# Expert slots in an order that the chip makes, weights waited for through ScalarE, and the first pass's transposes a block later

## What is computed

```python
h = layernorm(x)
q, k, v = h @ Wq, h @ Wk, h @ Wv                      # 8 heads of 64
q = softmax(q, over 64) * 0.125; k = softmax(k, over 4096)
out = (k v^T) applied to q, then @ Wo + bo
x = x + layernorm(out)
u = layernorm(x)
s = softmax(u @ centroids.T); top 2 of 16 -> gates g
routed = sum over the two experts of g * (u @ Wr[e].T + br[e])
shared = (u @ Ws[0].T + u @ Ws[1].T + sum(bs)) / 2
x = x + layernorm(u + routed + shared)
```

## Time and profile before

| what | value |
| --- | --- |
| median of 3 runs | 1136.12 us (1130.5 to 1185.25) |
| the profiled execution | 1130.6 us |
| its span, core 5, the slowest | 1128.7 us |
| the other cores' spans | 1099.4 to 1122.9 us |
| TensorE busy, matmuls | 833.8 us, 74% |
| VectorE, ScalarE, GpSimd busy | 587.4, 480.2, 273.7 us |
| mean granted TensorE clock, core 5 | 0.888 |

### The profile page before, as it was taken

One profiled execution on the slowest core, in us unless ns is written; L12 is line 12 of the kernel. 1 busy time (PEld: TensorE's weight loads), 2 busy tenths in 40 slices (PEclk: granted clock), 3 DMA queues, 4 the chain that ended last, 5 costly groups with the idle time before them and its releaser, 6 DMA issues.

```text
span 1128.7 us, 18028 instructions; the slowest of 8 cores (1099.4 to 1128.7 us)
## 1 busy us (share of the span) xinstructions
PE 833.8 (74%) x5008; PEld 410.9 (36%) x5008; DVE 587.4 (52%) x1352; ACT 480.2 (43%) x837; POOL 273.7 (24%) x295
## 2 busy tenths in 40 slices
PE   3797898888676677204377789964798978999994
PEld 1343444444233334102133345531344433444441
DVE  3589776776687888531032122210121233887876
ACT  1453454553676768300011222210121234777775
POOL 0132222213104343655011100010001004544441
PEclk9898999999889788556688999986999997999997
DMA  9999889867858992438979975677969655888885
GB/s 180 247 195 240 200 216 231 219 156 133 176 169 198 273 230 99 163 128 277 214 211 254 234 283 204 213 188 181 274 188 256 247 191 189 276 287 285 280 286 213
DMA packets 74194, 245.07 MB, mean 217 GB/s; under 512 B 9678, under 2 KB 9966, under 8 KB 73484
## 3 DMA queue, kind: packets, MB, share of 16 engines
q0 software_dynamic: 30800, 109.93, 42.6%
q1 hardware_dynamic: 43196, 132.88, 34.5%
HBM read 183.71 MB, written 98.19 MB: 250 GB/s over the span
## 4 chain that ended last, share of the span: by engine, by line
PE 34%; DMA 19%; DVE 18%; issue 10%; DVEq 7%; ACT 5%; ACTq 3%; POOLq 1%; another core or an unknown queue 1%; POOL 1%; SPq 0%
PE pa L1551 17%; DMA xs<-xd 5%; DMA wfull<-wr 4%; PE pa L554 3%; PE pa L480 3%; PE pa L1748 3%; DMA xh<-xin 2%; DMA out<-zo 2%; DVE xh L951 2%; PE pT L1514 2%; DVEq L590 2%; DVEq L356 2%; DMA xd<-ub,pos 2%; DVE acc L1788 1%; DVE acc L1779 1%
## 5 line engine op out<-in xcount | busy, mean ns | idle before, releaser
L1551 PE MATMUL pa<-wfull,xsT 128*128 128x512 bf16 x1200 | 287.8, 396 | 85.2 <-DMA wfull<-wr 49.1
L1583 DVE COPY ro<-pa 128x512 f32<-128x512 f32 x79 | 54.6, 691 | 319.5 <-PE pa L1551 308.2
L1551 PEld LDWEIGHTS pa<-wfull,xsT 128*128 128x128 bf16 x1200 | 116.9, 101 | 226.3 <-issue 111.3
L1582 ACT COPY ro<-pa 128x512 f32<-128x512 f32 x79 | 46.3, 587 | 274.6 <-PE pa L1551 256.4
L1748 PE MATMUL pa<-wfull,uT 128*128 128x512 bf16 x512 | 122.7, 383 | 0.0
L1765 POOL DMA_INDIRECT rr<-yr,ypos x64 | 84.4, 1318 | 155.6 <-issue 86.8
L1204 POOL DMA_INDIRECT xd<-ub,pos x64 | 63.3, 989 | 119.7 <-ACT ub L984 54.5
L918 PE MATMUL pa<-Mb,qT 128*128 128x512 bf16 x256 | 80.8, 446 | 0.0
L1436 POOL DMA_DIRECT2D wfull<-wr x28 | 14.8, 530 | 253.3 <-issue 169.8
L1530 ACT COPY xsT<-pT 128x1024 bf16<-128x1024 bf16 x40 | 40.5, 1013 | 81.0 <-PE pT L1514 78.0
L1514 PE MATMUL pT<-sq,xs 128*128 128x128 bf16 x608 | 47.6, 222 | 32.2 <-DMA xs<-xd 32.2
(11 more groups left out here) (208 smaller groups left out, 1347.9 us busy)
## 6 DMA issues: line engine op xcount, KB each, us to landing
yr<-ro SPq DMA_DIRECT2D x79, 512.0 KB, 4.1
xs<-xd SPq DMA_DIRECT2D x75, 256.0 KB
wfull<-wbf POOLq DMA_DIRECT2D x36, 512.0 KB, 13.6
xh<-xin SPq DMA_DIRECT2D x32, 512.0 KB, 14.7
stg<-wr POOLq DMA_DIRECT2D x32, 512.0 KB, 10.1
wbf<-stg SPq DMA_DIRECT2D x32, 512.0 KB, 10.6
wfull<-wr POOLq DMA_DIRECT2D x32, 512.0 KB, 16.3
out<-zo SPq DMA_DIRECT2D x32, 512.0 KB
```

What stands on the lines that cost most here:

```text
L1551: m = e.matmul(pa[j % 2][:, o * 512:(o + 1) * 512], xsT[j % 2][:, k * P:(k + 1) * P], wfull[:, c:c + 512], start=(k == 0), stop=(k == 7))
L1582: return e.copy(ro[j % 3][:, s], pa[j % 2][:, s])
L1583: return e.tensor_copy(ro[j % 3][:, s], pa[j % 2][:, s])
```

## The change

Line numbers in the order rows of the changed kernel are its own.

1. **Slot order.** The largest expert among 3 to 15 becomes a filler. Its weights stay in buffer 0 behind expert 0's; all others take turns between buffers 1 and 2. The others come in order, and each from the third on whose own slots are fewer than four (VISIT) is followed by so many of the filler's slots; what is left of the filler comes at the end. The table (ZY, TB) has a seventh number, the block of yr to which the slot's result goes, since the gathers still look for results in expert order.
2. **Loads.** One lookup for each slot (WL) in place of three; a float32 load goes out whole. Expert 1's load now stands in the second pass, expert 2's behind its last batches; zeroes for experts 8 to 15 are filled behind slot 0, and the zero tile is set by GpSimd.
3. **Waits for weights.** From slot 8 (NEAR) on ScalarE looks up what slot j + 1 waits for and waits for it (RD), ahead of its copy EO(j, 0); TensorE waits for RD and looks up the buffer alone.
4. **Slot 0** has a fixed place, waits for no table, and its matmuls come before slot 1's transposes.
5. **Stores** look up their block; unused slots store an old tile without waiting for copies. The last pass's first two blocks don't wait for the last stores.
6. **First pass.** TH and EH of the next group stand one V or Q block later, EU behind the third query block's VectorE work.

```diff
+VISIT = 4
+NEAR = 8
...
             TK(g, 2)
             if n:
                 H(n[1])
-                TH(n[0])
             X4(g, 1)
-            if n:
-                EH(n[0])
             EV(t[1])
 
             V(t[2])
             TK(g, 3)
             if n:
-                TH(n[1])
+                TH(n[0])
                 H(n[2])
-                EH(n[1])
+                EH(n[0])
...
             if n:
-                TH(n[2])
+                TH(n[1])
                 H(n[3])
-                EH(n[2])
+                EH(n[1])
...
             QQ(t[0])
             if n:
-                TH(n[3])
-                EH(n[3])
+                TH(n[2])
+                EH(n[2])
...
             QQ(t[1])
             if n:
+                TH(n[3])
+                EH(n[3])
                 E(g)
             else:
...
             QQ(t[2])
-            if n:
-                EU(g)
             QS(t[2])
             QR(t[1])
             QN(t[1])
+            if n:
+                EU(g)
...
+            if b == NB - 1:
+                plan[done].append((ZZ,))
+                plan[done].append((LD0, 2))
...
+            if s == NT - 1:
+                LD0(1)
     def ZZ():
         def zz(e):
-            wait(e, "W", 17)
+            wait(e, "W", NT - 1)
             return e.memset(zero[:], 0.0)
-        put("V", ("ZZ",), zz)
+        put("G", ("ZZ",), zz)
...
-            return e.tensor_copy(zidx[:], tmp)
+            return e.tensor_copy(zidx[:, 0:1], tmp[:, 0:1])
...
+            e.reduce_max(sc[0], key[:, 3:16], axis=AX.X)
...
+            e.tensor_scalar(one, key, sc[0], None, ALU.is_equal)
...
+            e.tensor_scalar(g, T, -1.0, float(VISIT), ALU.mult, ALU.add)
...
+            e.tensor_tensor_scan(hc[:, 3:17], ones16[:, 0:14], g[:, 2:16], 0.0, ALU.mult, ALU.add)
...
+            e.tensor_scalar(hc[:, 3:17], hc[:, 3:17], big_n, None, ALU.min)
...
+            e.scalar_tensor_tensor(tf[:, 1:2], sc[24], 0.0, sc[23], ALU.is_equal, ALU.mult)
+            e.scalar_tensor_tensor(tf[:, 5:6], sc[21], float(CAP), sc[24], ALU.mult, ALU.add)
+            e.scalar_tensor_tensor(tf[:, 6:7], sc[22], sc[24], sc[18], ALU.add, ALU.max)
+            dr()
+            return e.tensor_copy(tabi[:, 0:7], tf[:, 0:7])
         put("V", ("TB",), tb)
...
         def f(e):
             wait(e, "ZX")
             wait(e, "ZZ")
-            if n == 1:
+            if n:
                 wait(e, "TB")
-            if n >= 8:
+            if 8 <= n < NE:
                 wait(e, "ZF", n - 8)
             return [e.indirect_dma_start(
                 out=xd[:], out_offset=bass.IndirectOffsetOnAxis(ap=zidx[:, n:n + 1], axis=0),
                 in_=zero[:], in_offset=None, bounds_check=last_row[0], oob_is_err=False)]
-        put("G", ("ZF", n), f, f"d_zf{n % 8}")
+        put("G", ("ZF", n), f, f"d_zf{n % 8 if n < NE else 8}")
 
     def YP(n):
 
...
+        b = (0, 2, 1)[n]
+
         def f(e):
             if n == 0:
                 wait(e, "W", 15)
             if n == 1:
+                wait(e, "W", NT - 1)
+            if n == 2:
                 wait(e, "SCAT", batch_of[NT - 6])
                 wait(e, "TU", NT - 6)
-            if n == 2:
-                wait(e, "W", NT - 1)
-                for k in range(NE - 8, NE):
-                    wait(e, "ZF", k)
             if n:
                 for q in range(4 * n - 4, 4 * n):
                     wait(e, "PS", q)
-            return [e.dma_start(out=wfull[:, n * WSZ + h * QTR:n * WSZ + (h + 1) * QTR],
+            return [e.dma_start(out=wfull[:, b * WSZ + h * QTR:b * WSZ + (h + 1) * QTR],
                                 in_=(wbf if n else wr)[n][:, h * QTR:(h + 1) * QTR]) for h in range(4)]
-        put("G", ("LD0", n), f, f"d_v{n}" if n else "d_w0", 4)
-
-    def loads_until(n):
-
-        kind = [m for m in range(NE + 1) if (m in PRE or m == NE) == (n in PRE or n == NE)]
-        return sum(m <= n and m % 3 == n % 3 for m in kind)
-
-    def fetch(e, b, src, chan, part):
+        put("G", ("LD0", n), f, f"d_w{b}", 4)
...
-    def WL(j, h):
-
-        def f(e):
-            wait(e, "TB")
-            wait(e, "MM2", j - 1)
-            with from_table(nc, e, "Pool", tabi, j, ((2, NE - 1), (3, 2))) as ((reg, val), (buf, _)):
-                with e.If_ne(reg, 0):
-                    src = wr[bass.ds(val, 1), :, :].rearrange("a p c -> (a p) c")
-                    by_buffer(e, buf, lambda b: fetch(e, b, src, "d_w", (2 * h, 2 * h + 1)))
-        Q.own("G", f)
-
-    def WH(j):
+    def WL(j):
...
-            with from_table(nc, e, "Pool", tabi, j, ((4, NE), (3, 2))) as ((reg, val), (buf, _)):
-                with e.If_ne(reg, 0):
-                    src = wbf[bass.ds(val, 1), :, :].rearrange("a p c -> (a p) c")
-                    by_buffer(e, buf, lambda b: fetch(e, b, src, "d_v", range(4)))
+
+            def load(src, most):
+                with from_table(nc, e, "Pool", tabi, j, ((2, most), (3, 2))) as ((_, val), (buf, _)):
+                    weights = src[bass.ds(val, 1), :, :].rearrange("a p c -> (a p) c")
+                    by_buffer(e, buf, lambda b: fetch(e, b, weights, range(4)))
+            with from_table(nc, e, "Pool", tabi, j, ((2, NE),)) as ((some, _),):
+                with e.If_ne(some, 0):
+                    with from_table(nc, e, "Pool", tabi, j, ((4, 1),)) as ((prepared, _),):
+                        with e.If_eq(prepared, 0):
+                            load(wr, NE - 1)
+                        with e.Else():
+                            load(wbf, NE)
...
-                wait(e, "TB")
                 wait(e, "W", NT - 1)
                 wait(e, "SCAT", NB - 2)
                 wait(e, "SCAT", NB - 1)
+                wait(e, "ZF", 0)
+                return [e.dma_start(out=xs[0][:], in_=xd[0:P, :])]
+            wait(e, "TB")
+            wait(e, "ZF", NE)
             if j < NE:
-                wait(e, "ZF", j)
+                wait(e, "ZF", min(j + 1, NE - 1))
...
+    def arrival(e, j, b, first):
...
+        loads = ([(NE, 2)], [(v + 1, v // 2) for v in range(2, 15, 2)],
+                 [(v + 1, v // 2 + 1) for v in range(1, 14, 2)])[b]
+        for code, m in loads:
+            if code == NE or code <= j + 1:
+                with e.If_eq(first, code):
+                    e.wait_ge(Q.sem[f"d_w{b}"], 64 * m)
+
+    def RD(j):
+
+        def f(e):
+            with from_table(nc, e, "Activation", tabi, j, ((1, NE),)) as ((first, _),):
+                with e.If_ne(first, 0):
+                    with from_table(nc, e, "Activation", tabi, j, ((0, 2),)) as ((buf, _),):
+                        by_buffer(e, buf, lambda b: arrival(e, j, b, first))
+            e.sem_inc(Q.sem["rd"], 16)
+            return []
+        put("A", ("RD", j), f, "rd")
...
-            with e.If_ne(first, 0):
-                for n in range(b, min(NE, j + 1), 3):
-                    with e.If_eq(first, n + 1):
-                        e.wait_ge(Q.sem[f"d_v{b}" if n in PRE else f"d_w{b}"], 64 * loads_until(n))
+            if 0 < j < NEAR:
+                with e.If_ne(first, 0):
+                    arrival(e, j, b, first)
...
-            with from_table(nc, e, "PE", tabi, j, ((0, 3), (1, NE))) as ((buf, _), (first, _)):
+            if j == 0:
+                wait(e, "LD0", 0)
+                both(e, 0, None)
+                return
+            if j == 1:
+                wait(e, "TB")
+            if j >= NEAR:
+                wait(e, "RD", j)
+            cols = ((0, 3), (1, NE)) if j < NEAR else ((0, 3),)
+            with from_table(nc, e, "PE", tabi, j, cols) as regs:
+                buf = regs[0][0]
+                first = regs[-1][0]
...
+                if j == 2:
+                    for n in range(8, NE + 1):
+                        wait(e, "ZF", n)
             else:
                 wait(e, "YS", j - 3)
+            if j >= SURE:
+                wait(e, "EO", j - 3, o)
...
+            cols = ((6, NSLOT - 1), (0, 3)) if j >= SURE else ((6, NSLOT - 1),)
+            with from_table(nc, e, "SP", tabi, j, cols) as regs:
+                def rows():
+                    wait(e, "EO", j, 0)
+                    wait(e, "EO", j, 1)
+                    return e.dma_start(out=yb[bass.ds(regs[0][1], 1), :, :].rearrange("a p d -> (a p) d"),
+                                       in_=ro[j % 3][:])
+                if j < SURE:
+                    return [rows()]
+                seen = dict(Q.seen)
+                with e.If_ne(regs[1][0], 3):
+                    rows().then_inc(Q.sem[ys(j)], 16)
+                with e.Else():
+                    e.dma_start(out=yr[j * P:(j + 1) * P, :], in_=xh[j - SURE][:]).then_inc(Q.sem[ys(j)], 16)
+                Q.seen.clear()
+                Q.seen.update(seen)
+            return []
+        put("S", ("YS", j), f, ys(j))
...
     def experts():
-        for n in range(4):
+        ZF(0)
+        ZF(NE)
+        for n in range(1, 8):
             ZF(n)
-        LD0(1)
```

(25 more changed lines are left out.)

176 lines of the change are left out of this document (106 added, 70 removed).

## The result

The changed kernel takes 1083.7 us (median of 6 runs, 1078.9 to 1128.6), the kernel before beside it 1144.2 (6 runs). Some executions of either kernel are some per cent longer, with the cores of one die at a lower granted clock; the ratio is of the others alone, 0.954, interval 0.950 to 0.958: faster. The profiled execution took 1078.9 us, against 1130.6 before.

The account below looks back on a forecast made before the run. The slowest core, 5, sets the time; its longest stage, the expert slots, was split by transfers. 1130.6 - 8 - 4 - 32 - 5 = 1081.6, said as 1082 us; range 1038 to 1112.

Parts of the forecast that it names:

- Term 1: First pass: transposes a block later remove TensorE's waits for VectorE's normalised block; -8 us, bounds -20 and +5.
- Term 2: Table and first slots: table ready later, at about 503 us, but slot 1 earlier; -4 us, bounds -8 and +5.
- Term 3: Expert stage, slot 1 to last matmul: 402 us falls to 370 by the transfer split; -32 us, bounds -73 and +9.
- the check at expert 9: Expert stage: expert 9's load, needed four slots (15.6 us) after the request, takes 23 us including those slots' traffic.
- Term 4: Hand-over to the last pass: first blocks skip the store waits, GpSimd has fewer lookups; -5 us, bounds 0 and -9.
- ScalarE's lookups at nothing: Expert stage: a lookup is one register load and a branch, costed at nothing beside 1.1 of 3.9 us copying.
- holds the slot: Rival, expert stage: ScalarE's lookup delays the copy out of PSUM, 1.2 us for each of 67 slots; 1162 us, chance 0.07.
- Everything is covered: Rival, expert stage: TensorE bounds and all loads are hidden, -73 us there; 1040.6 us in all, chance 0.20.
- The transfers eat it: Rival: loads cost more, stage gains 0 to 15 us, first pass gains nothing; 1115 us, chance 0.15.
- the slower rival: Expert stage: ScalarE's lookup, at 4 us, adds 80 us over 67 slots; 1162 us, chance 0.07.
- The order isn't what I derived: Rival, slot table: one wrong column makes slots wait for other weights; would show as about 1115 us, no separate chance.

Follow-up runs that it names:

- a1_old_first: Changed kernel with the first pass put back in the old order; 0.982 of the kernel before, first pass 286.9 us against 270.8.
- early: Changed kernel with expert 2's first load moved behind zeroing of experts 1 to 7, and zeroing of experts 8 to 15 moved earlier; 0.958 of the kernel before.
- allbf: Changed kernel with the seven float32 loads fetching bfloat16 weights of the expert below; 0.923 of the kernel before, slots 329.0 us against 364.4.
- noload: Changed kernel without the expert loads behind the first three, every slot using buffer 0; one run, 1007.7 us, slots 292.3 us against 364.4.
- vlook: Changed kernel with the lookup of weights on VectorE instead of ScalarE; 0.958 of the kernel before, slots 366.6 us against 364.4.
- a4_no_visits: Changed kernel with VISIT = 0, all filler slots at the end; 0.987 of the kernel before, slots 395.0 us against 364.4.
- v5: Changed kernel with VISIT = 5 instead of 4; 0.959 of the kernel before, slots 362.8 us against 364.4.
- after_again: The changed kernel unchanged, run in a second batch; 0.956 of the kernel before, slots 365.0 us against 364.4.

## Why the prediction was right, and where not

I predicted 1082 us and it is 1083.7. Three of the four terms are right in kind. Terms 1, 2 and 4 were mis-sized, by -10.6, +5.9 and +2.0 us, and the errors nearly cancel: that the total is so close is in part luck. The forecast's own bounds, half of each term's, add up to 1051 and 1116, not to the 1055 and 1107 that I gave; the range of 1038 to 1112 was a choice beside them.

**Term 1, -8 predicted, -18.6 measured (a1_old_first: 16.1).** The mechanism was right. The step that failed is the size, "two thirds of 12.1": I summed the waits for hb alone, within 40 to 260 us of one core, and took a third off for the transfers. But a wait in an in-order queue also moves what stands behind it. On core 1 hb gave 11.0, the key transposes another 6.9, and the matmuls 3.2 (busy 220.0 to 216.8, fewer of them in slow stretches), less 1.2 for qn: 19.9 of 19.8. On core 5, from which the 12.1 was read, the pass is 14.4 us shorter. The third that transfers were to eat was not seen, and the fourth copy into hT, my bound of +5, made no new wait (1.4 us before and after). The bound of -20, "all waits, the slow matmuls and the stalls behind them", was the better figure.

**Term 2, -4 predicted, +1.9 measured.** The step that failed is that all of it was read from core 5, where the table was late before (44.4 us behind the second pass; 32.4 to 32.6 on cores 0 to 3). On core 5 slot 1 did come 9.3 us earlier. On cores 0 to 3 it came 5.9 us later, 57.4 to 63.3, because there GpSimd's list is the bound and the change put a memset, a load and another zeroing into it: the last scatter is issued 36 instead of 32 us behind the second pass, and slot 0's transposes start at 46.6 instead of 40.8. "Fit the 8.5 us in which GpSimd waited for the last positions" held for core 5 alone. The run early takes this back on such cores and so shows it. The table's own making was over-priced, too: 12.4 us were predicted, and it takes 9.3 to 10.8 by core, where it took 5.9 to 6.2. On core 5 it is ready no later than before, because the last positions came 3.9 us earlier (31.6 us behind the second pass for 35.5), which nothing in the term had foreseen.

**Term 3, -32 predicted, -31.4 measured.** The split holds on core 5, 498 to 865 us: transfers busy 0.84 of 367 us = 308 (307 predicted), the rest 59 (22 + 41 = 63 predicted). Pace and the sum of transfers were right, and so was the time of a load in the check at expert 9: 23 us predicted, and a float32 load with four slots beside it took 20.3 to 22.9 us. That makes a stop of 7.4 us, though, and at slot 26 of core 5, expert 9's, two copies are 16.8 us apart, a stop of 12.9. The prices of the two kinds of load don't follow from the earlier trace rows as written: 20.9 us for one of each and 164 for nine and seven give 8.9 and 12.0, not 7.4 and 13.5. The stated ones were the better: from the software queue's busy time within the slots in allbf (fourteen bfloat16 loads, 96 us without what noload has too) and in the changed kernel (141 us) they come to about 7 and 13. Two readings in the term were off. "Idle for float32 weights falls from 49 to about 40" named the wrong rows: the stop now shows as waits for rows, which share the transfer engines with the load and stand ahead of the matmuls on TensorE. And the stops last longer than their idle time, since the slot behind one runs at 1.2 GHz, 5.91 us for 3.62; I had no term for it. In the one stop shown the transfers were busy all the while (1.01 in 641 to 647 us), so it lies under their time there.

The weighed rule of the Trainium skill, DMA: Bandwidth & Descriptors (SWDGE vs HWDGE vs iDMA), by which a transfer engine takes turns between the software and the hardware queues, gave me 27 us for a float32 load beside full slot traffic. That took the turns to be equal in time. If they are counted in packets the trace agrees with the page: 576 and 590 packets beside that load (544 and 534 beside another, 544 to 562 us), of which the load's last 0.43 and the slots' 0.12 us, so that the load had 77% of the time. The load's own 22.7 us decide nothing: 13.5 + 4 x 2.4 = 23.1 comes out for any turns that let the slots' 9.6 us through before the load has ended. It is the rows' 15.2 to 18.9 us that show how the turns fall.

**Term 4, -5 predicted, -3.0 measured** (-4.2 at the gathers). The last pass's first transposes come 10.7 us after the last slot on core 5 (864.76 to 875.42) instead of 12.4, 1.7 us earlier:

```profile
865.55 0.23 PE L1732 MATMUL pa<-sq 128*128 128x128 bf16 x1 [0.80 <-issue]
875.42 1.86 PE L1829 MATMUL pT<-sq,ub 128*128 128x128 bf16 x16 [9.64 <-ACT ub L1817]
```

The step that failed is that "unused slots are stored without their copies" would free the way. The stores no longer wait for the copies, but the copies still stand in ScalarE's list ahead of ub, now with a table load each. Without the table loads the last matmul to the end takes 202.7 to 203.4 us, 4.3 to 5.0 less than before, which is the size predicted.

**ScalarE's lookups at nothing** was right for the slots and wrong for the work and for the hand-over: I listed a register load and a branch and missed 1.28 us per slot. With 1.1 us of copies that is 2.4 of 3.9 us, so it fits into a slot, and the rival "holds the slot" fell, as vlook and noload show. The Trainium skill has the reason in ScalarE activation tables: per-element evaluation and per-set limits (Table sets in the compiler and the runtime): the compiler places table loads per block. That a branch ends such a block is my inference. The trace agrees with it: 71 lookups, 71 loads, and in vlook and before none but the one at the program's start.

**The rivals.** "Everything is covered" put the slots at 329 us; only with half the bytes for seven loads (allbf) do they get there. "The transfers eat it" fell with a1_old_first, since a fuller first pass kept its gain, and with the loads' 20.3 to 22.9 us, which are the predicted 23. For the slower rival I had weighed the Trainium skill, Runtime: NRT & Kernel Launch (Instruction fetch mechanics), by which taken branches stall an engine. noload shows next to none of it on ScalarE: behind each of the 568 branches of its lookups (71 on each core), which jump over all the compares, the next instruction starts within 0.38 us, in the middle 0.11. "The order isn't what I derived" fell too: on core 5 the stops of experts 3, 9 and 15 stand at slots 6, 26 and 56 as in the list, those of experts 5 and 7 one and two slots ahead of it, where the rows are late.

## What to carry over

Moving work in an in-order queue: sum every wait that stands behind the stalled instruction on that engine, not only its own. With several cores, work a term out on an early and on a late core before it is taken for all. Slots put between loads brought 31 us (a4_no_visits); with transfers 0.93 busy, more of them (v5) only moved the stops. Then fewer bytes per load shorten the stops (allbf), and a request that is made earlier can push a more urgent one back (early). Work that hides in one stage can stand in the way at the hand-over to the next.

## What the runs showed of the hardware that I had not expected

- Lookups with branches on ScalarE bring an activation-table load of 1283 ns ahead of the next copy, 71 times, with no other function in between; on VectorE (vlook) nothing of the kind appears. It costs nothing that can be seen in the slots, and 1.3 to 2.0 us behind them.
- Rows of 256 KB take 2.5 to 3.1 us to land where only slots' traffic flies (core 1, 832 to 860 us) and 15 to 19 us beside a float32 load in the software queue, whose packets last over three times as long as theirs. Many stops begin with such a wait for rows.
- The slot behind a stop of 11 us took 2.3 us more than usual, at the granted clock of 0.50.
- On four of the eight cores the table is ready some 7 to 12 us later than on the others (cores 4 to 7 in the changed kernel's profile, 0 to 3 in after_again). The last positions are already late there, 31.6 to 33.7 us behind the second pass against 23.2 to 23.5. On core 5 VectorE stood still for 7.8 us until 458.19 ahead of one batch's positions, though the matmul that makes them had run at 450.6; on the early cores such a wait is 0.5 us. What holds it was not tried.
